# Moving small steps one to four units later in four stages of a fused four-layer kernel

## The chip, the cores and the metric

One NeuronCore of one Trainium2 chip runs the whole program. The metric is device time in microseconds (us) from launch to end; where several runs are given it is their median. The engines are TensorE (PE, with PEld for its weight loads), VectorE (DVE), ScalarE (ACT), GpSimd (POOL) and SyncE (SP, which here only issues transfers). Each runs its own program in order; they meet at semaphores.

## The reference

Four layers, each with an attention and a feed-forward part on x of 8 batches x 256 rows x 128 columns, each part behind a layer norm and added back to x. Cut to what matters here:

```
x = x + xattn0(norm(x), ctx)   # 16 heads of 64, bias per head, mask, softmax
x = x + ffn0(norm(x))          # 16 experts of 512, the best 4 of each row, exact gelu
x = x + xattn1(norm(x), ctx)   # 16 heads of 8, bias and mask, softmax
x = x + ffn1(norm(x))          # 8 routed experts and a shared one
x = x + retention2(norm(x), ctx); x = x + ffn2(norm(x))
x = x + xattn3(norm(x), ctx)   # 16 heads of 8, softmax
x = x + ffn3(norm(x))
# ffn0: sum over the 4 best experts e of gate[e] * (gelu(x@w1[e].T + b1[e]) @ w2[e].T + b2[e])
```

## The kernel before

x stays in SBUF for the whole program, as 16 tiles of 128 rows. A stage is written as one program for each engine (`tensor`, `scalar`, `vector`, `pool`, `sync`), and the programs of all stages are run one after the other on each engine. The order on an engine is therefore the order of the loops as written; a semaphore wait holds up everything behind it on that engine. A `Norm` object has five steps, each on its own engine: `stats` (DVE, L299 to L305), `power` (POOL, L310), `scale` (DVE, L330), `turn` (PE transposes, L339) and `copy` (ACT, L344, which signals `nrm_xt`).

**Wide attention (layer 0).** A unit u is a pair of heads of one batch; a batch b has 8 units (n = 0 to 7), and there are 64. PE's body for unit u is: `weigh(u)` (L1315, L1320, L1326), the first projection job of the next batch, `maxima` (L1306, odd n), `scores(u+3)` (L1291, L1296), `mix(u-2)` (L1345), the second job, `out` at n = 3 and 4 (L1368), `turn_out` (L1358). The jobs of the next batch are spread by `JOBS_AT`: two each at n = 0, 1, 2, 5, 6, 7, twelve in all (L1264, L1270). They share two banks; `wait_pr_free` lets a job start only when the job (or turn) two places earlier in that list has been read by ACT. ACT's body is: first job's evacuation (L1450 the float32 copy, L1451 the float16 one), `maxima` (L1456), `expo` (L1461 and L1463), second evacuation, `turn_out` (L1469), and at n = 7 the norm's `copy`. POOL's is: `split_` of the first job (L1210), `low(u)` (L1216, two), `split_` of the second. DVE's is: `weigh` (L1572), `scores` (L1553, four), `cut` for every other unit (L1561, L1563), `gather` (L1581 to L1587), the norm's steps near the end of a batch. PE's `maxima` waits for `cut`.

**First expert pair (feed-forward 0).** For each pair of experts there are 32 units of 128 hidden columns x 512 rows. PE's loop body is `up(u+4)` (L1825, three matmuls) and `down(u)` (L1888, twelve); ACT computes gelu twice (L1836), POOL takes the low half (L1859, `low`), DVE adds each finished output of four units to x (`adds`, L1971). `down(u)` of the first unit of output n (u = 4n) needs a free bank, that is `adds` of outputs 0 to n-2. Pair 0 also carries work left over from elsewhere: the last batch's norm (turned at u = 4, copied after gelu 8, then `halves`, L1725 and L1727, before low 9), the gate logits of the second half of the rows (`logits0`, L1747), their top 4 (`choose`, `weigh`, L1760 to L1811, on DVE), the turned gates (`turn_gates`, L1900, copied by ACT at L1951) and the product of gates and b2 (`bias2`, L1909), which DVE adds (L1988). `bias2(k)` for k of 1 or more waits until DVE has done `adds` of output 3+k and has added bias product k-1. `split` (L1734 to L1737) makes the float16 halves of the next pair's weights; `up(32)`, in the body of u = 28, needs them.

**Narrow attentions (layers 1 and 3).** Again 8 batches of 8 units. PE's body: `weigh(u)` (L735, L739), the norm's `turn` of batch b-2 (b of 2 and more, at n = 2), `maxima` (L725, odd n), `scores(u+3)` (L709, and L716 in layer 1), `mix` (L757), a job of the next batch (L684, L688 or L695, L698). DVE: `weigh` (L937, layer 1 only), `scores` (L920), `cut` (L927, L929), the norm's `scale` at n = 1, `norm_out` at n = 2 (L957, L960). `turn` and `maxima` write the same bank, so PE waits for ACT's copy one unit after the turn.

The lines that hold the orders of the first pair, on PE:

```
BIAS2 = {16: 0, 20: 1, 27: 2, 30: 3}
for u in range(TU):
    up(pe, 0, u + LAG)
    down(0, u)
    if u == 4:
        nm.turn(pe, B - 1, B, bank[SUMS])
    if u == 8:
        logits0(pe, 1, bank[TURNS])
    if u in TURN_GATES:
        turn_gates(TURN_GATES[u])
    if u in BIAS2:
        bias2(BIAS2[u])
```

Of the kernel before, what the change touches and what calls it, by code (L numbers as in the profile page):

```python
# [35 lines left out]
B = 8  # L36
# [99 lines left out]
def build(nc, io, out, upto=99):  # L136

    ctx = ExitStack()
    with ctx:
# [356 lines left out]
        def narrow_attention(layer, nm, late, ahead, after, lead):  # L496
# [79 lines left out]
            bq, bk, bv, bo = (far[f"b{c}{layer}"] for c in "qkvo")  # L576

            def job_bank(b, k):
                return bank[S_BANK[0] if b == 0 and k % 2 else PR]
# [81 lines left out]
            def tensor(pe):  # L661
# [135 lines left out]
                for u in range(B * PER_BATCH):  # L797
                    b, n = divmod(u, PER_BATCH)
                    weigh(u)
                    if b >= 2 and n == 2:  # L800
                        after.turn(pe, b - 2, b - 1, bank[TR])
                    if b >= 2 and n == 3:
                        pe.wait_ge(nrm_xt, after.ready(b - 2))
                    if n % 2 and u // 2 + 1 < B * GROUPS:
                        maxima(u // 2 + 1)
                    if u + AHEAD < B * PER_BATCH:
                        scores(u + AHEAD)
                    if u >= 2:
                        mix(u // 2 - 1, n % 2)
                    if u == 4:  # L810
                        row()
                    if b + 1 < B and n < JOBS:
                        project(b + 1, n)
                    if gated and b == B - 1 and n == 3:
                        pe.wait_ge(x_done, x0 + B - 2)
                        lead.gate.logits(pe, 0, bank[PR])
                    if b and n == 5:
                        out(b - 1)
# [5 lines left out]
            def scalar(act):  # L824
# [41 lines left out]
                for u in range(B * PER_BATCH):  # L866
# [4 lines left out]
                    if not masked and n % 2 and u // 2 + 1 < B * GROUPS:  # L871
                        maxima(u // 2 + 1)
                    if b >= 2 and n == 2:
                        after.copy(act, b - 2, b - 1, bank[TR])
# [144 lines left out]
        def wide_attention(nm, after, lead):  # L1019
# [35 lines left out]
            UNITS, QUADS = B * PAIRS, B * GROUPS  # L1055
            JOBS_AT = ((0, 1), (2, 3), (4, 5), (), (), (6, 7), (8, 9), (10, 11))
            OUT_AT = (3, 4)
            TURN_AT = NP - 1
# [127 lines left out]
            def pool(g):  # L1186
# [38 lines left out]
                for u in range(UNITS):  # L1225
                    b, n = divmod(u, NP)
                    jobs = JOBS_AT[n] if b + 1 < B else ()
                    for k in jobs[:1]:
                        split_(b + 1, k)
# [4 lines left out]
                    low(u)  # L1234
                    for k in jobs[1:]:
                        split_(b + 1, k)
# [5 lines left out]
            def tensor(pe):  # L1242
# [147 lines left out]
                for u in range(UNITS):  # L1390
                    b, n = divmod(u, NP)
                    jobs = JOBS_AT[n] if b + 1 < B else ()
                    weigh(u)
                    for k in jobs[:1]:
                        project(b + 1, k)
# [4 lines left out]
                    if u >= BEHIND:  # L1400
                        mix(u - BEHIND)
                    for k in jobs[1:]:
                        project(b + 1, k)
# [25 lines left out]
            def scalar(act):  # L1429
# [48 lines left out]
                for u in range(UNITS):  # L1478
                    b, n = divmod(u, NP)
                    jobs = JOBS_AT[n] if b + 1 < B else ()  # L1480
                    for k in jobs[:1]:
                        project(b + 1, k)
                    if n % 2 and u // 2 + 1 < QUADS:
                        maxima(u // 2 + 1)
                    expo(u)
                    for k in jobs[1:]:
                        project(b + 1, k)
# [164 lines left out]
        def experts0(nm, after, ahead):  # L1652
# [53 lines left out]
            COPY_GATES = {17: 0, 21: 1, 28: 2, 30: 3}  # L1706
            BIAS2 = {16: 0, 20: 1, 27: 2, 30: 3}

# [147 lines left out]
            def pool(g):  # L1856
# [5 lines left out]
                for u in range(TU):  # L1862
                    if u == 5:
                        nm.power(g, B - 1, B)
                    if u == 9:
                        halves(g, CHUNKS - 1)
# [12 lines left out]
            def tensor(pe):  # L1879
# [33 lines left out]
                for u in range(TU):  # L1913
# [3 lines left out]
                    down(0, u)  # L1917
                    if u == 4:
                        nm.turn(pe, B - 1, B, bank[SUMS])
                    if u == 8:  # L1920
                        logits0(pe, 1, bank[TURNS])
# [18 lines left out]
            def scalar(act):  # L1940
                for u in range(TU):
                    if u >= 2:
                        gelu(act, 0, u)
                    if u == 8:
                        nm.copy(act, B - 1, B, bank[SUMS])
# [1166 lines left out]
```

## Time and profile before

| | us |
|---|---|
| median of 3 runs | 1461.74 |
| lowest, highest | 1458.08, 1470.87 |
| the profiled execution, its own time | 1470.09 |
| its span, first to last instruction | 1468.3 |
| PE busy | 1320.7 (90%) |
| DVE, ACT, POOL busy | 1039.0, 899.1, 912.6 |
| mean granted clock of TensorE | 0.946 |

A profile shows one execution. Busy shares are means over stages with different limits, so each stage is read by itself: the timeline of each engine in order of time, with the idle time before an instruction and the one that ended it in square brackets; a table of stretches with the granted clock; and a list of who waited for whom. Merged rows stand for several instructions in a row (x12 is twelve), with the start of the first. Wide attention runs from about 43 to 379 us, the first expert pair from 379 to 442, the other pairs to about 740, the narrow attention of layer 1 from about 760 to 985, that of layer 3 from about 1250 to 1436.

### The profile page before, as it was taken

The numbers are of one execution on the slowest core, as the hardware profiler recorded it, in microseconds if no ns is written. First come the engines' busy times: TensorE is split into PE (matmuls) and PEld (weight loads), VectorE is DVE, ScalarE is ACT, GpSimd is POOL, SyncE is SP. The second block draws the span as 40 slices with busy tenths as digits, with TensorE's granted clock in tenths as the row PEclk, the third lists the DMA queues.
The fourth block names the chain that finished last, engine by engine and source line by source line (L and its number), as shares of the span: only waits on it lengthen the run. The fifth ranks groups of instructions, "written<-read, shape, count | busy, mean of one in ns | idle before, by whom it ended". The sixth has DMA issues, their size and how long they took to land.

```text
span 1468.3 us, 37233 instructions
## 1 busy us (share of the span) xinstructions
PE 1320.7 (90%) x14490; PEld 813.5 (55%) x14582; DVE 1039.0 (71%) x2493; ACT 899.1 (61%) x1487; POOL 912.6 (62%) x879
## 2 busy tenths in 40 slices
PE   5899999997889999999978998987989899799988
PEld 3466566665667777777733333433667466344435
DVE  7888888888655444444758899886788377677774
ACT  4677787774769999999834444432133333465555
POOL 6788887876658899989857566612353020655535
PEclk9999999999999999999969999997979699799998
DMA  8000000001013210000101211000000000000000
GB/s 275 9 9 9 9 9 9 2 2 32 14 34 99 62 46 14 29 29 26 55 4 34 65 34 33 31 1 29 1 2 10 1 1 1 8 9 5 5 2 30
DMA packets 26082, 39.64 MB, mean 27 GB/s; under 512 B 7314, under 2 KB 13364, under 8 KB 25428
## 3 DMA queue, kind: packets, MB, share of 16 engines
q1 hardware_dynamic: 25364, 35.58, 7.6%
q0 software_dynamic: 576, 2.10, 0.7%
q8 instruction: 97, 1.59, 0.4%
q14 instruction: 45, 0.37, 0.1%
HBM read 38.72 MB, written 1.05 MB: 27 GB/s over the span
## 4 chain that ended last, share of the span: by engine, by line
PE 60%; DVE 25%; issue 5%; POOL 5%; ACT 3%; DMA 1%; SPq 0%; POOLq 0%; DVEq 0%; ACTq 0%
PE bank L1888 10%; PE bank L1825 10%; DVE sbuf L920 6%; PE bank L757 4%; DVE sbuf L330 2%; PE bank L2359 2%; PE bank L1264 2%; PE bank L709 2%; PE bank L2117 2%; PE bank L1368 2%; POOL sbuf L1216 2%; DVE sbuf L937 2%; PE bank L2338 2%; PE bank L1345 2%; PE bank L1296 2%
## 5 line engine op out<-in xcount | busy, mean ns | idle before, releaser
L1836 ACT ACTIVATE sbuf<-bank,sbuf 128x512 f32<-128x512 f32 (+1 forms) x512 | 322.3, 684 | 26.1 <-PE bank L1825 13.8
L1859 POOL TENSOR_TENSOR sbuf<-sbuf 128x512 f16<-128x512 f32 x256 | 305.0, 1200 | 52.4 <-ACT sbuf L1836 51.3
L1888 PEld LDWEIGHTS bank<-sbuf 128*128 128x128 f16 x3072 | 193.9, 98 | 60.8 <-issue 1.1
L310 POOL TENSOR_TENSOR sbuf<-sbuf 128x2 f32<-128x2 f32 (+1 forms) x48 | 39.8, 828 | 291.6 <-DVE sbuf L305 286.8
L1888 PE MATMUL bank<-sbuf 128*128 128x128 f16 x3072 | 214.1, 220 | 0.3 <-DVEq L1976 0.3
L1825 PE MATMUL bank<-sbuf 128*128 128x512 f16 x768 | 209.8, 383 | 0.0
L920 DVE TENSOR_REDUCE sbuf<-bank 128x4 f32<-128x1024 f32 x128 | 156.4, 1222 | 58.4 <-PE bank L709 43.5
L1971 DVE SCALAR_TENSOR_TENSOR sbuf<-bank,sbuf 128x128 f32<-128x128 f32 x256 | 71.7, 341 | 163.2 <-PE bank L1888 163.1
L1216 POOL TENSOR_TENSOR sbuf<-sbuf 128x512 f16<-128x512 f32 x128 | 148.2, 1178 | 56.9 <-ACT sbuf L1463 56.8
L757 PE MATMUL bank<-sbuf 128*32 128x256 f32 x2048 | 141.0, 395 | 1.6 <-ACT sbuf L857 1.6
L1210 POOL TENSOR_TENSOR sbuf<-sbuf 128x512 f16<-128x512 f32 x96 | 110.4, 1166 | 23.0 <-ACT sbuf L1451 22.9
L857 ACT ACTIVATE sbuf<-sbuf 128x1024 f32<-128x1024 f32 x64 | 67.6, 1057 | 90.5 <-DVE sbuf L937 90.5
L1553 DVE CUSTOM_DVE_ANT_0 bank<-bank,sbuf 128x256 f32<-128x256 f32 x256 | 100.6, 454 | 23.1 <-PE bank L1296 23.0
L632 POOL TENSOR_TENSOR sbuf<-sbuf 128x512 f16<-128x512 f32 x64 | 66.5, 1040 | 71.9 <-ACT sbuf L836 71.9
L1461 ACT ACTIVATE sbuf<-sbuf 128x1024 f32<-128x1024 f32 x64 | 67.9, 1062 | 55.0 <-DVE sbuf L1572 54.8
L937 DVE TENSOR_TENSOR sbuf<-bank,sbuf 128x1024 f32<-128x1024 f32 x64 | 78.0, 1219 | 21.5 <-PE bank L739 21.2
L757 PEld LDWEIGHTS bank<-sbuf 128*32 128x32 f32 x2048 | 54.7, 111 | 66.3 <-issue 42.1
L1572 DVE TENSOR_TENSOR sbuf<-bank,sbuf 128x1024 f32<-128x1024 f32 x64 | 77.9, 1217 | 16.2 <-PE bank L1326 15.5
L857 ACT ACTIVATE sbuf<-bank 128x1024 f32<-128x1024 f32 x64 | 65.5, 1023 | 38.5 <-PE bank L739 38.2
L836 ACT ACTIVATE sbuf<-bank,sbuf 128x256 f32<-128x256 f32 x128 | 53.3, 469 | 58.2 <-PE bank L688 30.6
L1825 PEld LDWEIGHTS bank<-sbuf 128*128 128x128 f16 x768 | 65.2, 99 | 32.4 <-issue 1.9
L1450 ACT ACTIVATE sbuf<-bank 128x512 f32<-128x512 f32 x96 | 57.3, 597 | 37.5 <-PE bank L1264 22.6
(319 smaller groups left out, 2731.8 us busy)
## 6 DMA issues: line engine op xcount, KB each, us to landing
sbuf<-w SPq DMA_DIRECT2D x32, 256.0 KB, 2.9
sbuf<-bias_t SPq DMA_DIRECT2D x4, 1024.0 KB, 12.0
sbuf<-ctx_t SPq DMA_DIRECT2D x24, 128.0 KB, 2.4
sbuf<-bias_q POOLq DMA_DIRECT2D x4, 512.0 KB, 11.5
sbuf<-mask_t SPq DMA_DIRECT2D x8, 256.0 KB, 2.7
sbuf<-bias_t SPq DMA_DIRECT2D x8, 256.0 KB, 3.0
sbuf<-mask_q SPq DMA_DIRECT2D x8, 256.0 KB, 3.6
sbuf<-bias_q SPq DMA_DIRECT2D x8, 256.0 KB, 4.2
```

What stands on the lines that cost most here:

```text
L757: last = pe.matmul(bank[O_BANK[b % 2]][32 * j:32 * j + 32, part * S:part * S + S], lhs, exps[:, (2 * Q + j // 2) % EXPS, at:at + S], start ...
L857: act.activation(exps[:, u % EXPS, :], biased[:, u % 2, :] if masked else w_pair, ACT.Exp)\
L920: v.tensor_reduce(row_max[:, (u // 2) % 2, :, at].rearrange("p m j -> p j m"), s_pair.rearrange("p (j m c) -> p j m c", j=2, c=S), AX.X, A ...
L937: v.tensor_tensor(biased[:, u % 2, :].rearrange("p (j c) -> p j c", c=HW), w_pair.rearrange("p (j c) -> p j c", c=HW), add_t[u // PER_BATC ...
L1210: g.tensor_tensor(to[1], like(x32[:, k % 2, :], to[1]), to[0], ALU.subtract).then_inc(s["halved"], 1)
L1216: g.tensor_tensor(p_low[:, u % PROBS, cols], exps[:, u % 2, cols], p_high[:, u % PROBS, cols], ALU.subtract).then_inc(s["probs"], 1)
L1553: last = v.tensor_tensor_reduce(bank[S_BANK[j]][:, cols], bank[S_BANK[j]][:, cols], add_q[u // NP % 2][:, cols], 1.0, -BIG, ALU.add, ALU.m ...
L1572: v.tensor_tensor(biased[:, u % 2, :].rearrange("p (j c) -> p j c", c=HW), w_pair.rearrange("p (j c) -> p j c", c=HW), bias_t[:, 2 * n:2 * ...
L1825: last = pe.matmul(bank[u % 4][:, :], w1_16[p][:, w, f * P:(f + 1) * P], x16[:, xk, c * CHUNK:(c + 1) * CHUNK], start=k == 0, stop=k == 2)
L1836: last = act.activation(to, bank[u % 4][:, :], ACT.Gelu, bias=b1[p][:, f:f + 1], scale=1 / SCALE)
L1859: g.tensor_tensor(hid16[1][:, u % BUFS, :], hid[:, u % 4, :], hid16[0][:, u % BUFS, :], ALU.subtract)\
L1888: last = pe.matmul(bank[4 + out_no % 2][:, j * P:(j + 1) * P], hid16[h][:, u % BUFS, j * P:(j + 1) * P], w2_16[p][:, w, f * D:(f + 1) * D] ...
```

## The change

Nothing is added or removed; seven steps are issued at another place.
- Wide attention: at n = 0 both jobs of the next batch come at the place of the second one (`EARLY_JOBS`), on PE, ACT and POOL.
- First expert pair: `bias2(1)` from u = 20 to 24; the last norm's `turn` from 4 to 6 and its `copy` from gelu 8 to gelu 10; `halves` from low 9 to low 11; `logits0` from 8 to 9.
- Narrow attentions: for b = 2 to 6 `turn` and `copy` at n = 4 instead of 2, and PE's wait for the copy at n = 5 instead of 3. For b = 7 nothing changes.

```
+            def turned_at(b):
+                return 4 if b < B - 1 else 2
-                    if b >= 2 and n == 2:
+                    if b >= 2 and n == turned_at(b):
                         after.turn(pe, b - 2, b - 1, bank[TR])
-                    if b >= 2 and n == 3:
+                    if b >= 2 and n == turned_at(b) + 1:
                         pe.wait_ge(nrm_xt, after.ready(b - 2))
...
-                    if b >= 2 and n == 2:
+                    if b >= 2 and n == turned_at(b):
                         after.copy(act, b - 2, b - 1, bank[TR])
...
+            EARLY_JOBS = (0,) + (1,) * (PAIRS - 1)
...
-                    for k in jobs[:1]:
+                    for k in jobs[:EARLY_JOBS[n]]:
                         split_(b + 1, k)
...
-                    for k in jobs[1:]:
+                    for k in jobs[EARLY_JOBS[n]:]:
                         split_(b + 1, k)
...
-            BIAS2 = {16: 0, 20: 1, 27: 2, 30: 3}
+            BIAS2 = {16: 0, 24: 1, 27: 2, 30: 3}
...
-                    if u == 9:
+                    if u == 11:
                         halves(g, CHUNKS - 1)
...
-                    if u == 4:
+                    if u == 6:
                         nm.turn(pe, B - 1, B, bank[SUMS])
-                    if u == 8:
+                    if u == 9:
                         logits0(pe, 1, bank[TURNS])
...
-                    if u == 8:
+                    if u == 10:
                         nm.copy(act, B - 1, B, bank[SUMS])
```

The same two lines of jobs change in PE's and ACT's loops, with `project` for `split_`.

## Rows read from the trace of the kernel before

**Rows 1.** Who waited for whom on PE, 70 to 360 us: total, times, longest.
```profile
PE bank L1264 <- ACT sbuf L1451: 7.4, 5, 1.5
```

**Rows 2.** Timeline of PE, a batch boundary: start, us, engine, line, [idle before].
```profile
162.76 0.83 PE L1264 MATMUL bank<-sbuf 128*128 128x256 f16 x6 [1.48 <-ACT sbuf L1451]
163.52 0.39 PE L1291 MATMUL bank<-sbuf 64*128 64x256 f16 x4
...
165.01 0.82 PE L1264 MATMUL bank<-sbuf 128*128 128x256 f16 x6
```

**Rows 3.** Timeline of ACT, the same boundary.
```profile
164.59 1.06 ACT L1461 ACTIVATE sbuf<-sbuf 128x1024 f32<-128x1024 f32 x1
...
166.49 0.60 ACT L1450 ACTIVATE sbuf<-bank 128x512 f32<-128x512 f32 x1
```

**Rows 4.** Timeline of POOL, the same boundary.
```profile
164.04 2.24 POOL L1210 TENSOR_TENSOR sbuf<-sbuf 128x512 f16<-128x512 f32 x2
```

**Rows 5.** Timeline of DVE, the two steps of the cut, twice.
```profile
166.16 0.19 DVE L1561 TENSOR_SCALAR sbuf<-sbuf 128x8 bf16<-128x8 f32 x1
166.38 0.19 DVE L1563 SCALAR_TENSOR_TENSOR sbuf<-sbuf 128x8 bf16<-128x8 f32 x1
...
175.53 1.00 DVE L1561 TENSOR_SCALAR sbuf<-sbuf 128x8 bf16<-128x8 f32 x1
176.56 1.09 DVE L1563 SCALAR_TENSOR_TENSOR sbuf<-sbuf 128x8 bf16<-128x8 f32 x1
```

**Rows 6.** Timeline of PE, first expert pair, around the turn.
```profile
383.99 0.83 PE L1888 MATMUL bank<-sbuf 128*128 128x128 f16 x12
...
385.31 0.83 PE L1888 MATMUL bank<-sbuf 128*128 128x128 f16 x12
388.46 0.44 PE L339 MATMUL bank<-sbuf 128*128 128x128 f32 x2 [2.32 <-DVE sbuf L330]
```

**Rows 7.** Timeline of POOL, first expert pair.
```profile
386.06 4.49 POOL L1859 TENSOR_TENSOR sbuf<-sbuf 128x512 f16<-128x512 f32 x4
```

**Rows 8.** Timeline of PE, first expert pair, around bias2(1).
```profile
412.96 0.83 PE L1888 MATMUL bank<-sbuf 128*128 128x128 f16 x12
418.68 2.04 PE L1909 MATMUL bank<-sbuf 16*128 16x128 f32 x8 [4.89 <-DVE sbuf L1988]
...
428.26 0.60 PE L1900 MATMUL bank<-sbuf 128*16 128x128 f32 x4
...
433.18 1.15 PE L1909 MATMUL bank<-sbuf 16*128 16x128 f32 x8
```

**Rows 9.** Stretches of the first pair: length, busy of five engines, PEclk, DMA.
```profile
418.70:425.60 6.90, 6.90 (x38) 5.02 (x39) 0.00 (x0) 2.15 (x4) 1.15 (x1) 0.51 0.18 67
```

**Rows 10.** Timeline of DVE, first expert pair: gate steps, adds, bias.
```profile
412.80 0.29 DVE L1806 TENSOR_TENSOR sbuf<-sbuf 128x128 f32<-128x128 f32 x1
413.12 1.16 DVE L1807 TENSOR_TENSOR sbuf<-sbuf 128x128 f32<-128x128 f32 x1
...
416.56 1.13 DVE L1971 SCALAR_TENSOR_TENSOR sbuf<-bank,sbuf 128x128 f32<-128x128 f32 x4
417.85 0.69 DVE L1988 TENSOR_TENSOR sbuf<-sbuf,bank 128x512 f32<-128x512 f32 x1 [0.16 <-DVE sbuf L1971]
```

**Rows 11.** Timeline of DVE, first expert pair: first and last of four split steps.
```profile
429.03 0.42 DVE L1734 TENSOR_SCALAR sbuf<-sbuf 128x512 f16<-128x512 f32 x1
...
431.39 1.65 DVE L1737 SCALAR_TENSOR_TENSOR sbuf<-sbuf 128x512 f16<-128x512 f32 x1
```

**Rows 12.** Timelines of PE and DVE, layer 1, unit 2 of a batch.
```profile
881.94 0.44 PE L339 MATMUL bank<-sbuf 128*128 128x128 f32 x2 [0.99 <-DVE sbuf L330]
...
883.28 1.23 DVE L920 TENSOR_REDUCE sbuf<-bank 128x4 f32<-128x1024 f32 x1 [0.26 <-PE bank L716]
```

**Rows 13.** Timelines of PE and DVE, layer 3, units 4 and 2.
```profile
1339.60 0.39 PE L709 MATMUL bank<-sbuf 32*128 32x256 f16 x4 [0.30 <-DVE sbuf L920]
...
1334.19 1.23 DVE L920 TENSOR_REDUCE sbuf<-bank 128x4 f32<-128x1024 f32 x1 [0.86 <-PE bank L709]
```

More of the change, by code:

```diff
@@ L1393, in tensor @@
                     weigh(u)
-                    for k in jobs[:1]:
+                    for k in jobs[:EARLY_JOBS[n]]:
                         project(b + 1, k)
@@ L1401, in tensor @@
                         mix(u - BEHIND)
-                    for k in jobs[1:]:
+                    for k in jobs[EARLY_JOBS[n]:]:
                         project(b + 1, k)
@@ L1480, in scalar @@
                     jobs = JOBS_AT[n] if b + 1 < B else ()
-                    for k in jobs[:1]:
+                    for k in jobs[:EARLY_JOBS[n]]:
                         project(b + 1, k)
@@ L1485, in scalar @@
                     expo(u)
-                    for k in jobs[1:]:
+                    for k in jobs[EARLY_JOBS[n]:]:
                         project(b + 1, k)
```

## The prediction

> **What bounds the kernel now.** I read the list of waits of PE first, then PE's timeline at each place that the change touches, then the engine named in the bracket there, back to what held it. The reader is to look for three things: the idle time in brackets, whether the engine that ended it was itself waiting, and which work of PE stands ready behind the stall.
>
> In wide attention PE loses 7.4 us in five equal waits, all before the first job of a batch [rows 1]. Each is 1.48 us: PE has finished `weigh` at 162.76 - 1.48 = 161.28 and cannot start job 0 until ACT has evacuated job 11 [rows 2]. Behind that job stand `scores` and `mix`, which need nothing from it.
>
> In the first expert pair PE stops twice. Before the turn it is idle for 2.32 us, until DVE has scaled [rows 6]. Before bias2(1) it is idle for 4.89 us [rows 8]: DVE is in a row of gate steps, then `adds` of output 4, then the first bias product [rows 10]. After this gap the granted clock is 0.51, the lower level (1.2 GHz), for about 7 us [rows 9]. In the narrow attentions the turn at unit 2 stands ahead of `scores`: in layer 1 PE waits 0.99 us for it and DVE then waits 0.26 us for the scores [rows 12]; in layer 3 DVE waits 0.86 us [rows 13].
>
> **The change part by part.** *Wide attention, jobs at the end of unit 0.* No instruction is added. With `scores` and `mix` ahead (165.01 of the second job less 163.52 of the scores, 1.49 us [rows 2]) PE reaches job 0 at 161.28 + 1.49 = 162.77, where job 11 is read at 162.76 in any case. The 1.48 us are filled, and everything behind is earlier by that. Five boundaries give 5 x 1.48 = 7.4 us; the first batch, the next boundary and the last show no such wait, so nothing is taken there. What is late next: on ACT job 0's evacuation now follows the exponentials. Before, they began at 164.59 and the next evacuation at 166.49, 1.90 us later [rows 3]. Without job 0's evacuation ahead of them they can begin 1.5 us earlier, at 163.1, end at 165.0, and job 0 is read at about 165.9. PE wants that bank for job 2, which began at 167.6 in its timeline and now could at 166.1. That is a margin of 0.2 us only; I take it as holding. POOL gets low(0) ahead of two splits; it had a full queue here (two splits, 2.24 us [rows 4]) and keeps it.
>
> The unknown cost is a collision. The cut's two steps took 0.19 us each in one place and 1.00 and 1.09 in another [rows 5]; the long ones ran beside POOL's subtractions, the short ones at a gap of POOL. The difference is 1.71 us. The cut of unit 0 was a short one; 1.5 us earlier it falls beside the splits of rows 4. The cut of unit 2 was a long one and may become short. So a boundary is worth between 1.48 - 1.71 and 1.48 + 1.71 us; I take 1.48, since DVE has idle time there and one cut may lose what the other wins. All five together: -1.2 to 16 us.
>
> The Trainium skill, on the page "SBUF — State Buffer", section "SBUF: two separate sides", says that GpSimd and a DVE instruction with two SBUF inputs or in a two-port mode exclude each other for a whole instruction. By that rule this edit, which closes POOL's gap beside the first cut, gives the lower end; it is the last rival below. The rows of the cut agree with the rule; how often it strikes after the change they cannot show.
>
> *First pair, the norm.* PE's gap begins at 386.14. With the turn at u = 6 two more units stand ahead of it, 1.32 us each (385.31 less 383.99 [rows 6]), and scaling is done at 388.46, when PE gets there. But down(5) needs low(5), and POOL starts that at 386.06 behind the norm's power and needs 4.49 / 4 = 1.12 us for it [rows 7]; PE, with up(9) done at about 386.8, waits 0.4 us there. Gain 2.32 - 0.4 = 1.9 us. The copy stands two gelus later and the halves two lows later, as the turn does; `up` of that quarter comes at u = 16 only, so they are hidden by some 10 units, 13 us. `logits0` one unit later waits for nothing: its copy follows gelu 10, before PE's up(13) is done. DVE takes the logits a little earlier than before, with PE.
>
> *First pair, bias2(1).* The gap goes as long as what PE does in place of it is ready. PE's idle time begins at 418.68 - 4.89 = 413.79. Units 21 to 23 and up(28) take 3 x 1.32 + 0.65 = 4.6 us, to 418.4; down(24) needs `adds` of output 4, which end at 416.56 + 1.13 = 417.69 [rows 10]. Margin 0.7 us. bias2(1) then comes after down(24) and the turned gates, at about 419.5, and needs DVE's bias product, ready at 417.85 + 0.69 = 418.54 [rows 10]. Both sides are earlier by the 1.9 us of the norm, so the margins stay. The gap's 4.89 us go. With them goes the low clock: from 418.68 to 428.26 PE did one bias product and four units in 9.58 us; at full clock they are 1.15 (the product at 433.18 [rows 8]) + 4 x 1.32 = 6.43 us. That is 3.15 us more. Next in line is `split`, which stands on DVE behind the bias add: it took from 429.03 to 433.04 [rows 11], 4.0 us. Added to a bias product ending at 420.6 and its add of 0.69 that is 425.3; PE reaches up(32) at about 426.1. Margin 0.8. Sum of the pair: 1.9 + 4.9 + 3.15 = 10.0 us. Behind u = 32 the pair runs without a wait on PE, so this is kept to the end. Bounds: if the seven short gate steps (0.29 us) all become long (1.13 to 1.16 [rows 10]), DVE is 5.9 us later, 5.2 us of gap remain at down(24) and the clock falls again: 10.0 - 5.2 - 3.15 = 1.6 us. Above: 2.32 + 4.89 + 3.15 = 10.4.
>
> *Narrow attentions, turn at unit 4.* DVE sets the pace. In layer 1 its 0.26 us go; the turn at unit 4 stands ahead of `scores` again, but PE, freed of 0.99 us of waiting and 0.44 of turning [rows 12], arrives early. I take 0.26 for each of five batches: 1.3 us. In layer 3 at unit 4 PE had 0.30 us to spare [rows 13]; the turn takes 0.44. Of the 0.86 us at unit 2 I take the turn's 0.44: 5 x 0.44 = 2.2 us. Bounds for both layers: 5 x 2 x -0.44 = -4.4, if DVE waits for the turn in the new place, and 5 x (0.26 + 0.86) = 5.6. PE's wait for the copy moves with it, and ACT still copies right after the exponentials of the same unit; nothing more is queued behind. POOL's `halves` of batch b-3 come a batch later and stay covered.
>
> **The sum.** 7.4 + 10.0 + 1.3 + 2.2 = 20.9 us. The profiled execution, 1470.1 us, would become 1449.2. It lies 8.4 us above the median of the three runs; I take the gain off that median: 1461.7 - 20.9 = 1440.8 us, 1.4% less. The three runs of one kernel span 12.8 us, so about 1% (14.6 us) is what a measurement here tells from no change.
>
> **The rivals.** *A. The wait is renamed in the pair.* down(24) waits for the same `adds` that held bias2(1). It decides when DVE's gate steps lose more than the 0.7 us of margin. At its full price the pair gives 1.6 us: total 12.5, time 1449.2. For it: the steps are already long five times of twelve by my count of the timeline. Against it: POOL's gap beside the early ones comes from ACT loading tables, which stays. *B. The wait is renamed in wide attention.* Job 2 waits for job 0's evacuation, with 0.2 us to spare. If it costs what the old wait did, 7.4 us are lost: total 13.5, time 1448.2. Against it: ACT starts its exponentials about 1.5 us earlier than before. *C. It does not reach the end.* The narrow attentions give nothing or lose 4.4: total 13.0 to 17.4, time 1444.3 to 1448.7. *D. Slower.* POOL and DVE exclude each other in all of units 0 to 2, where POOL now has no gap. Both cuts long and, at the same price, one more two-port step (the mask) is 1.71 + 1.1 = 2.8 us more on DVE per boundary; it decides when this exceeds the 1.48 us won. Price 5 x (2.8 - 1.48) = 6.6 us lost, and the same exclusion takes the pair to 1.6 and the narrow layers to 0: 5.0 us slower, 1466.7. By the page's rule named above this is how it comes out if every such pair overlaps.
>
> **How the numbers follow.** Forecast (20.9, from 15 to 27 by the collisions) 0.66; A 0.10; B 0.10; C 0.09; D 0.05. The forecast's own lower end, with the scatter of runs, leaves 0.04 inside 1%. A and B lie within 1%; C is split. So: faster 0.69, same 0.28, slower 0.03. The range: 1434 adds half of the first part's upside (4.3) and the narrow layers' (2.1) to the forecast; 1456 takes in A to C with the scatter of the median. D is left out, as is the upper 16 us of the first part: together under 2 in 10.
>
> **What would show it.** After the change: no bracket before L1264 at a batch's start, and each of the middle batches shorter by about 1.5 us; before the turn in the pair no 2.3 us gap but one of 0.4 before an L1888; no gap before the second bias product and a granted clock of 1.00 behind it; DVE's bracket before L920 at unit 2 gone in layers 1 and 3. Wrong would be: a wait of PE on L1451 at job 2, on L1563 over 1 us at unit 1, on L1971 before down(24), or a new bracket before L920 at unit 4.

## The result and the profile after

| kernel | median us (lowest to highest, runs) | ratio to the kernel before, 95% interval |
|---|---|---|
| before | 1463.85 (1458.08 to 1470.87, 8) | |
| after | 1454.88 (1453.71 to 1458.88, 8) | 0.9928 [0.9903, 0.9953] |

The change makes the kernel 9.0 us faster by the medians (0.6%), 0.7% by the ratio. Its interval leaves out 1, but the gain is under the 1% that the prediction took for the least that counts, where 20.9 us (1.4%) had been forecast. The profiled execution after took 1458.9 us, the longest of its eight, and its span is 1457.1 us.

From here on a stage's length is the distance of two DVE instructions that exist in every kernel: `weigh(u)` of wide attention (L1572 before, L1577 after), `adds` of the first pair (L1971, L1976) and `scores` of the narrow layers (L920, L924), all counted from 0 in order of time (of `adds` the merged rows). "A middle batch" is from `weigh(8b+6)` to `weigh(8b+14)`, for b = 1 to 5 (the boundaries to batches 2 to 6).

| stretch | before | after | gain | forecast |
|---|---|---|---|---|
| wide: `weigh(0)` to `weigh(3)` | 14.28 | 15.35 | -1.07 | 0 |
| wide: `weigh(6)` to `weigh(14)` | 39.62 | 40.16 | -0.54 | 0 |
| wide: five middle batches | 5 x 41.29 | 5 x 40.92 | 1.85 | 7.4 |
| last `weigh` of layer 0 to adds 1 of the pair | 27.74 | 24.21 | 3.53 | 1.9 |
| pair: adds 3 to adds 5 | 18.28 | 9.80 | 8.48 | 8.05 |
| pair: adds 5 to adds 8 | 19.30 | 19.61 | -0.31 | 0 |
| layer 1: scores 15 to 59 | 155.31 | 154.08 | 1.23 | 1.3 |
| layer 3: scores 16 to 56, five batches | 5 x 21.77 | 5 x 21.52 | 1.3 | 2.2 |

The gain up to adds 1 is not the edit's alone: the granted clock moved there too, as the experiments show.

**In the first pair both gaps went.** Timeline of PE after, at the places of [rows 6] and [rows 8]:

```profile
385.62 0.84 PE L1893 MATMUL bank<-sbuf 128*128 128x128 f16 x12 [0.48 <-POOL sbuf L1864]
...
387.62 0.39 PE L339 MATMUL bank<-sbuf 128*128 128x128 f32 x2
...
415.38 0.60 PE L1905 MATMUL bank<-sbuf 128*16 128x128 f32 x4
415.91 1.15 PE L1914 MATMUL bank<-sbuf 16*128 16x128 f32 x8
```

The 2.32 us before the turn have gone, and the small wait for `low(5)` is there: 0.48 us, where 0.4 had been worked out. The second bias product has no bracket (4.89 us before). Stretches of the pair after (length, busy of the five engines, granted clock, DMA), to be held against the 0.51 of [rows 9]:

```profile
400.00:407.00 7.00, 7.00 (x77) 5.29 (x76) 3.52 (x14) 6.91 (x11) 3.45 (x4) 1.00 0.01 2
407.00:414.00 7.00, 7.00 (x86) 5.23 (x84) 6.79 (x10) 7.00 (x14) 6.64 (x6) 1.00 0.26 83
414.00:421.00 7.00, 7.00 (x73) 5.14 (x71) 4.65 (x11) 5.76 (x11) 5.25 (x6) 1.00 0.34 90
```

PE is busy throughout and keeps the upper clock level (1.00, 2.4 GHz).

**Wide attention gave nothing.** The wait of [rows 1] is gone from the list of waits on PE (60 to 365 us: total, times, longest), and a larger one has come:

```profile
PE bank L1311 <- ACT sbuf L1474: 11.0, 19, 0.9
```

L1311 is PE's `maxima`, L1474 is ACT's copy of `turn_out`. The two share bank TR, so `maxima` of the next unit stands until ACT has read the transposes. In the kernel before, the same pair had 1.4 us in 7 waits of at most 0.2. Part of the 11.0 is a wait renamed: on DVE's cut (L1563) `maxima` lost 7.0 us in 8 waits before, and 3.9 in 3 after. A middle boundary after, PE's timeline (cf. [rows 2]):

```profile
246.04 1.48 PE L1269 MATMUL bank<-sbuf 128*128 128x256 f16 x12
247.36 0.60 PE L1363 MATMUL bank<-sbuf 128*128 128x128 f32 x4
...
249.41 0.83 PE L1269 MATMUL bank<-sbuf 128*128 128x256 f16 x6
250.97 0.27 PE L1311 MATMUL bank<-sbuf 128*128 128x128 bf16 x2 [0.72 <-ACT sbuf L1474]
```

Both jobs and the transposes (L1363) follow without a gap; the stall stands one unit later. ACT, the same boundary after:

```profile
245.88 0.38 ACT L344 ACTIVATE sbuf<-bank 128x256 f32<-128x256 f32 x1
246.38 1.06 ACT L1466 ACTIVATE sbuf<-sbuf 128x1024 f32<-128x1024 f32 x1
247.35 1.04 ACT L1468 ACTIVATE sbuf<-sbuf 128x1024 f16<-128x1024 f32 x1
248.29 0.58 ACT L1455 ACTIVATE sbuf<-bank 128x512 f32<-128x512 f32 x1
248.77 0.59 ACT L1456 ACTIVATE sbuf<-bank 128x512 f16<-128x512 f32 x1
249.25 0.60 ACT L1455 ACTIVATE sbuf<-bank 128x512 f32<-128x512 f32 x1
249.73 0.61 ACT L1456 ACTIVATE sbuf<-bank 128x512 f16<-128x512 f32 x1
250.21 0.62 ACT L1474 ACTIVATE sbuf<-bank 128x512 f32<-128x512 f32 x1
251.94 0.60 ACT L1455 ACTIVATE sbuf<-bank 128x512 f32<-128x512 f32 x1 [1.12 <-POOL sbuf L1215]
```

ACT has no gap but the hand-over at 246.3 from the norm's copy to the end of `turn_out`: exponentials, two evacuations, copy. ACT, not PE, sets the pace here. The same piece of work in the kernel before had one gap of ACT, ahead of job 0:

```profile
162.59 0.38 ACT L344 ACTIVATE sbuf<-bank 128x256 f32<-128x256 f32 x1
163.62 0.60 ACT L1450 ACTIVATE sbuf<-bank 128x512 f32<-128x512 f32 x1 [0.65 <-PE bank L1264]
...
167.44 0.62 ACT L1469 ACTIVATE sbuf<-bank 128x512 f32<-128x512 f32 x1
```

From the norm's copy to the start of `turn_out`'s it was 167.44 - 162.59 = 4.85 us, after it is 250.21 - 245.88 = 4.33. So the move can only bring the 0.5 us that ACT's gap of 0.65 leaves, whatever PE saves. The second thing to see is the bracket of 1.12: ACT's next evacuation waits for POOL. `x32` has two places, so job 2's float32 copy needs POOL's split of job 0, and POOL now has `low(0)` ahead of it:

```profile
248.47 2.27 POOL L1221 TENSOR_TENSOR sbuf<-sbuf 128x512 f16<-128x512 f32 x2
250.69 3.57 POOL L1215 TENSOR_TENSOR sbuf<-sbuf 128x512 f16<-128x512 f32 x3
```

The collision of the cut came too; both steps are long where they were 0.19 each in [rows 5]:

```profile
247.87 0.62 DVE L1566 TENSOR_SCALAR sbuf<-sbuf 128x8 bf16<-128x8 f32 x1
248.52 1.15 DVE L1568 SCALAR_TENSOR_TENSOR sbuf<-sbuf 128x8 bf16<-128x8 f32 x1
```

It ended at 249.67, 1.3 us before PE's `maxima` began, and so cost nothing here.

**Batch 0 loses.** It had no wait to remove, but gets the new order. PE and ACT after, batch 0:

```profile
49.49 0.83 PE L1269 MATMUL bank<-sbuf 128*128 128x256 f16 x6 [0.57 <-ACT sbuf L1456]
53.44 0.39 PE L1325 MATMUL bank<-sbuf 64*128 64x512 bf16 x2 [1.06 <-ACT sbuf L1461]
```
```profile
52.03 0.60 ACT L1455 ACTIVATE sbuf<-bank 128x512 f32<-128x512 f32 x1 [1.62 <-PE bank L1269]
```

This is a line to be read with care: it names PE's job as the releaser, but that job began at 49.49 and takes 0.83, so it had long been done. The split of job 0, which began on POOL at 50.77, is what ended just then. PE's 1.06 is for the shift copy (L1461), which stands on ACT behind this evacuation.

**Layer 3.** DVE and POOL after, unit 2 of a batch (cf. the 0.86 of [rows 13]; the last line is the next `scores`):

```profile
1344.57 1.23 DVE L924 TENSOR_REDUCE sbuf<-bank 128x4 f32<-128x1024 f32 x1
1345.83 0.18 DVE L931 TENSOR_SCALAR sbuf<-sbuf 128x8 bf16<-128x8 f32 x1
1346.05 1.16 DVE L933 SCALAR_TENSOR_TENSOR sbuf<-sbuf 128x8 bf16<-128x8 f32 x1
...
1349.22 1.22 DVE L924 TENSOR_REDUCE sbuf<-bank 128x4 f32<-128x1024 f32 x1
```
```profile
1346.00 1.15 POOL L640 TENSOR_TENSOR sbuf<-sbuf 128x512 f16<-128x512 f32 x1
```

DVE before, the same unit:

```profile
1355.99 1.23 DVE L920 TENSOR_REDUCE sbuf<-bank 128x4 f32<-128x1024 f32 x1 [0.86 <-PE bank L709]
1357.25 0.62 DVE L927 TENSOR_SCALAR sbuf<-sbuf 128x8 bf16<-128x8 f32 x1
1357.91 0.20 DVE L929 SCALAR_TENSOR_TENSOR sbuf<-sbuf 128x8 bf16<-128x8 f32 x1
...
1360.13 1.21 DVE L920 TENSOR_REDUCE sbuf<-bank 128x4 f32<-128x1024 f32 x1
```

The bracket is gone and this `scores` comes 0.74 us earlier in the batch (12.17 instead of 12.91 after the batch's first). But the cut's second step now begins beside a POOL subtraction and takes 1.16 instead of 0.20 (the first takes 0.18 instead of 0.62), so the next `scores` is 4.65 us behind instead of 4.14: only 0.2 of the 0.74 remains.

### The profile page after: what moved, and what is told of

The parts are those of the page before. It is cut to its first block, busy times and chain, and to the rows that moved or that the text cites. A ratio compares the mean times of both kernels' runs of the same rounds, so it can differ in the third digit from the quotient of the medians.

```text
span 1457.1 us, 37325 instructions
## 1 busy us (share of the span) xinstructions
PE 1321.0 (91%) x14582; PEld 808.9 (56%) x14582; DVE 1044.4 (72%) x2493; ACT 898.3 (62%) x1487; POOL 910.6 (62%) x879
## 4 chain that ended last, share of the span: by engine, by line
PE 56%; DVE 26%; issue 7%; POOL 5%; ACT 5%; DMA 1%; SPq 0%; POOLq 0%; DVEq 0%; ACTq 0%
PE bank L1893 11%; PE bank L1830 10%; DVE sbuf L924 6%; PE bank L761 4%; DVE sbuf L330 3%; PE bank L2364 2%; DVE sbuf L941 2%; PE bank L713 2%; POOL sbuf L1221 2%; PE bank L2122 2%; PE bank L1373 2%; PE bank L2343 2%; DVE sbuf L1577 2%; DVE bank L1558 1%; PE bank L720 1%
## 5 line engine op out<-in xcount | busy, mean ns | idle before, releaser
L1864 POOL TENSOR_TENSOR sbuf<-sbuf 128x512 f16<-128x512 f32 x256 | 304.1, 1198 | 41.6 <-ACT sbuf L1841 40.4
L310 POOL TENSOR_TENSOR sbuf<-sbuf 128x2 f32<-128x2 f32 (+1 forms) x48 | 40.4, 841 | 297.2 <-DVE sbuf L305 292.4
L924 DVE TENSOR_REDUCE sbuf<-bank 128x4 f32<-128x1024 f32 x128 | 156.3, 1221 | 52.9 <-PE bank L713 38.5
L1976 DVE SCALAR_TENSOR_TENSOR sbuf<-bank,sbuf 128x128 f32<-128x128 f32 x256 | 71.8, 342 | 152.4 <-PE bank L1893 152.2
L1577 DVE TENSOR_TENSOR sbuf<-bank,sbuf 128x1024 f32<-128x1024 f32 x64 | 77.9, 1217 | 17.6 <-PE bank L1331 16.8
L330 DVE TENSOR_SCALAR sbuf<-sbuf 128x128 f32<-128x128 f32 x112 | 70.9, 693 | 11.3 <-POOL sbuf L310 11.2
## 6 DMA issues: line engine op xcount, KB each, us to landing
sbuf<-bias_q POOLq DMA_DIRECT2D x4, 512.0 KB, 11.4
```

The lines of the kernel that those rows point to most:

```text
L330: last = v.tensor_scalar(self.tile(k)[:, j, :], x[:, t, :], mv[:, t, 0:1], rstd[:, t:t + 1], ALU.subtract, ALU.mult)
L924: v.tensor_reduce(row_max[:, (u // 2) % 2, :, at].rearrange("p m j -> p j m"), s_pair.rearrange("p (j m c) -> p j m c", j=2, c=S), AX.X, A ...
L1864: g.tensor_tensor(hid16[1][:, u % BUFS, :], hid[:, u % 4, :], hid16[0][:, u % BUFS, :], ALU.subtract)\
```

## The experiments

All times are medians; the ratio is to runs of the kernel before made between them on the same chip (medians 1463.85 for the first four, 1464.20 for the next four, 1465.84 for the last). The three groups ran on three chips, so between groups the ratios compare better than the medians.

| run | edits | median us (lowest to highest) | ratio, 95% interval |
|---|---|---|---|
| e1_wide | wide | 1463.18 (1456.73 to 1471.98) | 1.0000 [0.9971, 1.0029] |
| e2_pair | norm, bias | 1461.32 (1450.48 to 1465.44) | 0.9957 [0.9926, 0.9988] |
| e4_no_wide | norm, bias, narrow | 1454.67 (1453.32 to 1458.26) | 0.9941 [0.9920, 0.9962] |
| e5_pe_only | as e4, wide on PE alone | 1455.27 (1454.29 to 1456.67) | 0.9934 [0.9913, 0.9956] |
| e3_narrow | narrow | 1464.33 (1458.28 to 1466.92) | 0.9987 [0.9966, 1.0007] |
| e9_bias_only | bias | 1458.63 (1451.16 to 1464.11) | 0.9950 [0.9926, 0.9974] |
| e6_pool_back | as e4, wide on PE and ACT | 1453.63 (1449.39 to 1455.86) | 0.9923 [0.9899, 0.9948] |
| e8_turn_first | as e6, `turn_out` first | 1456.84 (1449.28 to 1461.53) | 0.9937 [0.9911, 0.9964] |
| e10_spread | as e4, jobs spread from b = 2 | 1449.50 (1448.08 to 1451.36) | 0.9891 [0.9873, 0.9909] |
| e12_from_b2 | as e6, from b = 2 | 1452.15 (1449.96 to 1456.03) | 0.9907 [0.9888, 0.9926] |
| e13_norm_only | norm | 1466.07 (1461.78 to 1470.12) | 1.0000 [0.9984, 1.0016] |
| e14_before_again | none | 1462.17 (one run) | |

### Which part moves the time

e1_wide has only the `EARLY_JOBS` lines of the diff, e2_pair only those of the first pair, e3_narrow only `turned_at`; e4_no_wide is the changed kernel without `EARLY_JOBS`.

> The wide attention's edit alone, on the kernel before. Theory Q (queue): with POOL's low(0) ahead of the split of job 0, ACT cannot evacuate job 2 (the float32 copy has two buffers, and job 2 needs that of job 0), so nearly all of the 1.48 us comes back one unit later; the stage gains 0 to 0.5 us and the whole is within 2 us of before. Forecast: 7.4 us faster. Rival C (collisions): the same 0 for the whole, but by long cut steps on DVE, with PE's waits before L1311 ended by L1568 and not by ACT.

> The four edits of the first expert pair alone. Theory: they are nearly all of the gain; PE's offset against before reaches 11 to 12 us at the pair's end, and the median is 8 to 12 us below before's. Forecast of the prediction: 10.0 us.

> Only the narrow attentions' edit. My theory (the narrow edit is real but smaller than forecast): in layer 1 the stretch of five middle batches is 1.2 us shorter, in layer 3 about 1.2 us shorter in all, so 2.5 to 3 us in the profile, with the wide attention and the first pair as before. Rival C of the prediction (the narrow layers give nothing, DVE waits for the turn in its new place): 0 or slower, with a bracket before DVE's scores at unit 4. A third possibility, that the whole of the measured 9 us is the narrow edit and the pair gives nothing: 7 us or more below the kernel before.

> The change without its wide attention edit (pair and narrow edits kept). Theory Q: same time as the changed kernel within 1.5 us, since the wide edit is worth nothing: 10 to 13 us below before in its profile. Forecast: 7.4 us slower than the changed kernel.

Wide attention alone gives nothing (1.0000, to 0.3% by the interval), and taking it away from the changed kernel changes nothing (1454.67 and 1454.88). In e1's profile the stretches are those of the table above: `weigh(0)` to `weigh(3)` 15.34, then 40.15, then five times 40.92. In the nine profiles with the old order in batch 0 the first of these was 13.65 to 14.29. So 1.1 to 1.7 us are lost in batch 0, 0.54 at the next boundary, and 5 x 0.37 = 1.85 won: nil. The 9 us come from the other parts. The narrow edit alone cannot be told from nothing in the medians (0.9987 [0.9966, 1.0007]), but its stretches repeat in every profile: 154.08 us in layer 1 for 155.31, 104.2 for 105.0 in the later part of layer 3. e2_pair won 10 us in its profiled first pair and only 2.5 in the median, where 8 to 12 had been expected; this comes up again at the end of the next part.

### The bias product and the norm

```
e9:  BIAS2 = {16: 0, 24: 1, 27: 2, 30: 3}
e13: turn 4 -> 6, copy 8 -> 10, halves 9 -> 11, logits0 8 -> 9
```

> Only bias2(1) from unit 20 to 24. My theory (the gap and the slow clock behind it are real cost, and nothing gives it back): the stretch of the first pair from the 3rd to the 5th output's adds is shorter by 7.4 to 8.5 us, no gap of PE ahead of the second bias product and no stretch at a granted clock near 0.5 behind it, and the median is 7 us or more below the kernel before. Rival (the gain is given back later, since the two pair edits together gained 10 us in their profile and only 2.5 us in the median): the stretch is shorter by the same 8 us, the median by 3 us or less.

> Only the norm's turn, copy, halves and logits of the first pair, one to two units later. Theory (a real gap that the granted clock can hide): the gap before the turn is gone; where the granted clock stays at 1.00 ahead of it, the first adds come 1.9 us earlier, and where it falls for some 3 us at 376 to 380, as in four of the earlier runs, nothing is gained, since TensorE is late anyway. Median 0 to 2 us below the kernel before. Rival (the forecast's 1.9 us in every execution): median 2 us or more below.

> The kernel before, unchanged, for a second profile. Theory (TensorE's granted clock falls or stays up at the same places from one execution to the next, and this moves stages that the change does not touch): wide attention's middle batches 41.29 us again and the gap before the second bias product again within 0.3 us of 4.89 with a granted clock near 0.5 behind it, while the start, the retention, the stretch at 366 to 380 us and the last 45 us differ by 1 to 4 us from the first profile. Rival (the profile of before is typical in all of its stages): every stage within 0.3 us of the first profile, and the whole within 1 us of it.

From adds 3 to adds 5 the five profiles with the old bias place took 18.28 (before), 17.25 (e1), 17.18 (e3), 17.56 (e13) and 18.81 (before again), mean 17.8; every kernel with the new place took 9.80 or 9.81. That is 8.0 us, as forecast (7.4 to 9.0 from profile to profile). e9's profile has the second bias product with no bracket, and the second profile of before has the old one again:

```profile
415.26 1.15 PE L1909 MATMUL bank<-sbuf 16*128 16x128 f32 x8
```
```profile
416.20 2.04 PE L1909 MATMUL bank<-sbuf 16*128 16x128 f32 x8 [4.88 <-DVE sbuf L1988]
```

0.31 us come back between adds 5 and 8 (19.61 for 19.30, in all kernels with this edit). The median fell by 5.6 us against 1464.20, and by the interval 3.8 to 10.8: less than the theory's 7, more than the rival's 3; the interval takes in the first and leaves out the second.

The norm's edit is worth nothing in the median. The gap before the turn is not a fixed 2.32 us: in the second profile of before it was

```profile
385.99 0.44 PE L339 MATMUL bank<-sbuf 128*128 128x128 f32 x2 [0.75 <-DVE sbuf L330]
```

and in e9, which still has the turn at unit 4, there was none. What differs ahead of it is the granted clock. Stretches of the first profile of before, then of the second:

```profile
367.00:371.00 4.00, 3.85 (x32) 2.28 (x33) 3.30 (x16) 1.84 (x4) 2.45 (x2) 0.57 0.41 124
375.00:379.00 4.00, 2.39 (x37) 2.02 (x36) 2.52 (x11) 2.05 (x5) 2.03 (x2) 1.00 0.00 0
```
```profile
367.00:371.00 4.00, 4.00 (x30) 2.71 (x27) 3.66 (x7) 2.99 (x6) 2.45 (x2) 1.00 0.42 133
375.00:379.00 4.00, 3.31 (x17) 2.27 (x16) 3.70 (x9) 3.06 (x6) 1.98 (x2) 0.66 0.00 0
```

Where the clock falls some 12 us after the last `weigh` (before again, e1, e2, e3, e9, e13, e10), PE reaches the turn late and DVE is ready or nearly so: the edit then removes a gap that is small or absent. From the last `weigh` of layer 0 to adds 1 it was 26.1 us in e1, e3 and before again without the edit, 25.2 in e2 and e13 with it, but 25.3 in e9 without it. So it brings 0 to 1 us there. The 24.2 to 24.3 us of after, e4, e5, e6, e8 and e12 are this edit together with a clock that stayed up; no profile shows the old order with a clock up in both stretches, so the full 1.9 us were not isolated.

### Wide attention: which engine's order

The three programs can be moved one at a time, since only semaphores tie them. e5 moves the jobs on PE alone, e6 on PE and ACT; POOL keeps the split of job 0 ahead of `low(0)`:

```
 # PE (e5, e6) and ACT (e6)
-for k in jobs[:1]:
+for k in jobs[:(0 if n == 0 else 1)]:
```

> As e4, with the wide edit on PE alone; ACT and POOL keep their old order. Theory Q: the 1.48 us wait before job 0 is filled and job 0's split stays ahead of low(0), so ACT's evacuation of job 2 does not wait; each boundary from the third on is 1.0 to 1.5 us shorter, no loss in the first two batches, 5 to 7 us less than e4. Rival C (collisions on the cut): no more than 0.4 us a boundary, as in the changed kernel.

> The changed kernel with POOL's order of the kernel before in wide attention; TensorE's and ScalarE's jobs stay at the end of the first unit. Theory 'POOL's queue': the wait of ScalarE on POOL's split of job 0 before the evacuation of job 2 goes, and each middle boundary gains 1.0 us or more over the kernel before. Theory 'ScalarE's own queue' (turn_out's copy stands behind exponentials and two evacuations, and maxima waits for it): ScalarE's wait on the split goes, but TensorE's wait on turn_out's copy stays over 1 us, and a boundary gains 0.2 to 0.4 us, as with TensorE's order alone; the median stays within 2 us of the changed kernel's.

PE's idle brackets of one middle batch (`weigh(22)` to `weigh(30)`), all that PE's timeline lists but one of 0.15 marked "issue", beside the length of that batch:

| kernel | before job 0 | job 2 | `maxima`, n = 7 | n = 1 | n = 3 | sum | batch |
|---|---|---|---|---|---|---|---|
| before | 1.48 | 0 | 0.20 | 0 | 0.66 | 2.34 | 41.29 |
| after | 0 | 0 | 0.20 | 0.72 | 0.90 | 1.82 | 40.92 |
| e6_pool_back | 0 | 0 | 0.20 | 0.72 | 0.68 | 1.60 | 40.69 |
| e8_turn_first | 0 | 0.54 | 0.19 | 0 | 1.56 | 2.29 | 41.20 |
| e10_spread | 0 | 0 | 0.19 | 0.51 | 0 | 0.70 | 39.66 |

The batch follows the sum, to 0.15 us. With PE alone (e5) a batch is 41.12 us, 0.17 less than before where 1.0 to 1.5 had been expected, and `weigh(3)` to `weigh(6)` and `weigh(6)` to `weigh(14)`, expected without a loss, are 0.64 and 1.26 us longer. The wait for `turn_out`'s copy is longest there:

```profile
169.79 0.27 PE L1310 MATMUL bank<-sbuf 128*128 128x128 bf16 x2 [1.36 <-ACT sbuf L1473]
```

ACT still had its gap ahead of job 0 there (0.64 us). With ACT moved too, e6:

```profile
168.37 0.27 PE L1310 MATMUL bank<-sbuf 128*128 128x128 bf16 x2 [0.72 <-ACT sbuf L1473]
```

ACT's wait on POOL before job 2 is gone in e6, ACT works without a gap but the hand-over up to that copy, and the 0.72 stay: this is what isolates ACT's queue. Each batch is 0.23 us shorter than after, 0.59 shorter than before. So POOL's order costs 0.23 us a boundary, and the larger part of the loss (1.48 - 0.59) is ACT's queue. My first theory, that POOL's queue is the cause, holds for the smaller part only. Neither theory had the size: 0.59 lies between the 1.0 or more of POOL's queue and the 0.2 to 0.4 of ACT's. The median of e6 cannot be told from that of after.

### ACT's queue: another order, or less in it

e8 puts `turn_out` ahead of both jobs at n = 0, on PE and ACT. e10 keeps the order of after, and takes work out of ACT's unit 0 from batch 2 on, where ACT has gaps later. e12 is e6 from batch 2 on.

```
 # e8, PE and ACT
+if n == 0 and u // 2 >= 2:
+    turn_out(u // 2 - 2)
 for k in jobs[(0 if n == 0 else 1):]:
     project(b + 1, k)
 # e10: one job at n = 0, one at n = 3
 JOBS_AT = ((0, 1), (2, 3), (4, 5), (), (), (6, 7), (8, 9), (10, 11))
+SPREAD  = ((0,), (1, 2), (3, 4), (5,), (), (6, 7), (8, 9), (10, 11))   # b >= 2
 # e10 on PE, ACT and POOL; e12 on PE and ACT
+for k in jobs[:(0 if n == 0 and b >= 2 else 1)]:
```

> As the run before, and at the first unit of a batch turn_out (transposes on TensorE, copy on ScalarE) goes ahead of both jobs. Theory 'ScalarE's own queue': TensorE's wait on turn_out's copy before maxima goes, a middle boundary gains 1.0 to 1.5 us over the kernel before, the five 5 to 7 us, and the median is 4 to 7 us below that of the kernel without the wide edit (1454.7), near 1449. Rival (ScalarE is full through the whole boundary, so any order ends with the same late piece): TensorE's wait moves to the evacuation of job 0 before job 2 or to the exponentials, and the boundary gains 0.5 us or less.

> Pair and narrow edits as in the changed kernel; in wide attention, from batch 2 on, only job 0 stands at the end of the first unit, and jobs 1 to 5 come one place later (one at unit 0, two each at units 1 and 2, one at unit 3). Theory 'ScalarE is the bound of the boundary': with 0.96 us of evacuation less in the first unit, turn_out's copy is done before TensorE wants it, the 0.72 us wait before maxima goes, and a middle batch takes 39.9 to 40.4 us (41.29 in the kernel before, 40.92 in the changed one, 40.70 with POOL's order back); the median is 1449 to 1452. Rival (DVE or POOL bounds the batch as a whole, and any relief at unit 0 is lost by unit 4): a middle batch stays at 40.6 us or more.

> The kernel with POOL's order back, with the moved jobs only from batch 2 on, so that the first two boundaries are those of the kernel before. Theory: the 0.65 us lost in batch 0 and the 0.55 us at the next boundary come back, each of five middle boundaries gains 0.59 us as in the run with POOL's order back, and the median is 2.5 to 3.5 us below that of the kernel without the wide edit (1454.7), near 1452. Rival (the wide stage's gain does not reach the end because the granted clock in later stages takes it): the stage is 2.9 us shorter and the median 1454 or more.

e8 falls to its rival: the wait at n = 1 goes, but 0.54 comes before job 2 and 1.56 at n = 3, and the batch is 41.20. This other order of the same ACT work only moves the late piece. POOL has a part in it: it stands idle 1.46 us for the later evacuation of job 0, has no gap of 0.1 us in the 17 us after that, and ACT waits for its splits three times in this batch (0.35, 0.22, 0.38), the last time one evacuation ahead of the copy that ends the 1.56:

```profile
176.73 0.60 ACT L1456 ACTIVATE sbuf<-bank 128x512 f32<-128x512 f32 x1 [0.38 <-POOL sbuf L1214]
```

e10 takes one job out of unit 0, on ACT an evacuation of 0.48 + 0.48 us from start to start. ACT there:

```profile
202.91 0.58 ACT L1459 ACTIVATE sbuf<-bank 128x512 f32<-128x512 f32 x1
203.39 0.59 ACT L1460 ACTIVATE sbuf<-bank 128x512 f16<-128x512 f32 x1
203.87 0.60 ACT L1478 ACTIVATE sbuf<-bank 128x512 f32<-128x512 f32 x1
```

`turn_out`'s copy follows the one evacuation directly, and PE:

```profile
204.61 0.27 PE L1315 MATMUL bank<-sbuf 128*128 128x128 bf16 x2 [0.51 <-ACT sbuf L1478]
```

The wait did not vanish, because PE too has a job less ahead of it; but the one at n = 3 did, and a middle batch is 39.66 us: 1.63 less than before, more than the theory's 39.9 to 40.4 and more than the 1.48 of the removed stall. Relief gives what no order gave. It fits ACT as the bound, but does not prove it by itself, since PE has a job less and POOL a split less in that unit as well; e6 is what tells the engines apart. The five batches bring 8.1 us in the profile. The last units of the stage give 0.6 back (38.86 for 38.24 us from `weigh(56)` to `weigh(63)`). The median of 1449.50 is 5.4 us below that of after, and the ratio of 0.9891 [0.9873, 0.9909], where after has 0.9928, makes it the lowest of the study: 1.1% faster than before (five runs; the two intervals overlap by 0.0006). e12 gave 5 x 0.59 and a median of 1452.15, as expected; its bare gain over e4 is 2.5 us, on another chip, and 5.0 by the ratios, whose intervals overlap a little too.

### The clock

Two stretches of the tail of the program, with the same work of all engines ahead of them, in e4 (tail 41.99 us, from the last `scores` of layer 3 to the end):

```profile
1405.50:1409.50 4.00, 2.56 (x37) 1.08 (x40) 3.46 (x5) 2.32 (x3) 0.02 (x1) 1.00 0.00 0
...
1413.50:1417.50 4.00, 3.64 (x53) 1.53 (x56) 1.93 (x8) 2.05 (x2) 0.70 (x1) 1.00 0.00 0
```

and in e2 (tail 44.69 us):

```profile
1412.10:1416.10 4.00, 2.56 (x36) 1.08 (x40) 3.45 (x5) 2.32 (x3) 0.01 (x1) 1.00 0.00 0
...
1420.10:1424.10 4.00, 4.00 (x25) 2.00 (x29) 1.33 (x6) 1.02 (x1) 0.56 (x1) 0.50 0.00 0
```

The first rows are alike to a hundredth in time; in the second, 4 us behind the end of the first, e2 is at the lower level and has done 25 matmuls where e4 has done 53. It costs 2.7 us. e9 and e13 show the same long tail (44.7); before and the kernels that hold all of norm, bias and narrow edits do not (41.9 to 42.2), nor do e3 (42.1), before again and e1 (41.0). Between the two profiles of before, whose spans differ by 7.9 us, the start differs by 0.9, the way to adds 1 by 1.6, the end of retention by 0.8, two stretches of feed-forward 2 by 1.5 and 2.1, layer 3's first half by 1.0, the tail by 1.0; wide attention from `weigh(3)` to `weigh(56)` differs by 0.03.

## Why the prediction was wrong

**The sum was 20.9 us, the time fell by 9.0.** By its terms:

*Wide attention, 7.4: this step failed.* The stall went as said, and PE filled it with `scores` and `mix`. The step "what is late next" followed ACT only to the evacuation of job 0 and found a margin of 0.2 us for job 2. In the middle batches that held: job 2 has no bracket (in batch 0 it has one of 0.57). But ACT's body goes on, and its last piece in unit 0 is `turn_out`'s copy, whose bank `maxima` needs. From the norm's copy over exponentials and two evacuations to the start of this copy ACT takes 4.33 us with no gap but 0.1 us. ACT could give only its own gap of 0.65 us, so a boundary was worth 0.5 to 0.6 at most (e6: 0.59). Rival B had the engine right and the place wrong, with a chance of 0.10.

*"POOL ... had a full queue and keeps it"*: this is the second part of the failure. The queue was as full, but its order changed, and job 2's evacuation waits for the split of job 0 through the two places of `x32`. Price 0.23 us a boundary (e6 against after), which leaves 0.37 of 1.48.

*"Nothing is taken" in the first batches.* I took a boundary without the old stall to cost nothing in the new order. It cost 1.1 to 1.7 us in batch 0 and 0.54 at the next, and cancelled the 1.85 won. e12, which leaves them out, got it back.

*Collisions, -1.2 to 16 us.* The short cut did become long (0.62 and 1.15), but it was hidden. Rival D's overlap did happen in wide attention, and did not reach the end there.

*Pair, bias product, 4.9 + 3.15 = 8.05: right.* Measured 8.0 in the profiles, less 0.31 given back. The margins held: no bracket of PE on `adds`, the clock at 1.00. Rival A did not occur.

*Pair, norm, 1.9: mis-sized, one execution's gap taken as the value.* It was read from one execution in which the clock happened to be up at 375 to 379. In others the gap was 0.66 to 0.75 or absent, and the edit alone gave 1.0000 [0.9984, 1.0016].

*Layer 1, 1.3: right* (1.23). *Layer 3, 2.2: mis-sized.* The bracket went, 0.74 us of it was passed on, and 0.5 was lost to the cut's second step beside POOL, 1.16 for 0.20. About 0.2 to 0.25 remain for each batch, 1.3 in all. The Trainium skill, page "SBUF — State Buffer", section "SBUF: two separate sides", says that GpSimd and a DVE instruction with two SBUF inputs, as this step is, shut each other out for a whole instruction; the rows here agree (1.16 beside, 0.20 else), and this is the one place of the change where it was seen to cost time.

Put together: 0 (wide) + 8.0 - 0.3 + 0 to 1 (norm) + 1.2 + 1.3 = 10.2 to 11.2 us by the profiles, against 9.0 in the medians (6.9 to 14.2 by the interval). The rest is within what the clock moves from run to run.

**What stays open.** Why e2's median is only 2.5 us lower (6.3 by the ratio, 1.8 to 10.8 by its interval), with 10.0 us less from the last `weigh` to adds 5 than in the second profile of before (50.99 for 60.94). Its profile gives the gain back later: against the first profile of before it is 11.4 us ahead behind the pair and 7.5 at the end, with 2.7 lost in the tail and 1.5 in the second half of feed-forward 2; against the second it is 9.4 ahead behind the pair and 0.4 behind at the end, with 3.6 lost in the tail. The mean granted clock, which is known for every run, says that the other runs are like it: in eight of e2's twelve it was 0.944 to 0.949, and these took 1460.6 to 1465.4 us, median 1461.8; ten of the 35 runs of before had such a clock, and they took 1468.7 to 1474.9, median 1471.4. At a like clock e2 is thus 9.6 us shorter, near the 10.0 forecast for the pair; it was granted less of it in most runs (the median of before had 0.952). What decides the clock's fall at those places was not found.

## What to carry to other kernels

When a stall of one engine is filled, follow the engine that caused it to the last piece of its loop body, and add up its work without gaps: it can come forward only by its own idle time, here 0.65 us of 1.48, and the other order of the same work that was tried did not help. Taking one piece out of that unit, on all three engines, did, and made 0.59 us a boundary into 1.63. Apply a reorder only where the stall is (here from batch 2 on), and move a program's order on each engine by itself: a buffer of two places tied ACT to POOL's order, at 0.23 us a boundary.

## What the runs showed of the hardware

The granted clock of TensorE takes its two levels at different places in executions of one and the same kernel (0.57 and 1.00 at 367 to 371 us in the two profiles of before), and in different kernels behind the same work. The stages that it touches moved by 2 to 5 us over the fourteen profiles (the tail 41.0 to 44.7, the end of retention 51.3 to 55.9, the time to `weigh(3)` 57.5 to 59.3 in the kernels that leave batch 0 as it was), while wide attention from `weigh(3)` to `weigh(56)` took 267.6 to 267.7 us in all seven profiles with the old order throughout (before, before again, e2, e3, e4, e9, e13). A stall that the clock hides in one execution and not in another (0, 0.75 and 2.32 us before the same turn) should be costed from more than one profile. Other falls come every time: behind the gap of 4.9 us before the second bias product the mean granted clock of the next 7 us was 0.50 to 0.68 in all five profiles that have the gap (4.88 or 4.89 us), and 1.00 in all nine that have none.
